# Both multi-head attentions of a four-layer gated network: head turns moved from TensorE to VectorE, the maxima's rows written by small DMAs

## The reference, cut to what matters

```
layer 0, feed-forward part: a mixture of M = 2 self-attentions (mha_wq/wk/wv/wo, biases bq, bk, bv, bo),
  for each m:  q = n1 @ wq + bq;  k = n1 @ wk + bk;  v = n1 @ wv + bv          (16 heads x 16)
               p = softmax(q k^T * scale);  o = (p v) @ wo + bo
  out = base + sum_m probs[m] * o_m        probs = softmax(mean over tokens of n1 @ rw + rb)
  then a router picks 2 of 8 experts for the batch
layer 2, cross attention: q from x, k and v from the context, keys masked (key_padding_mask),
  p = softmax(q k^T * scale + mask);  out = (p v) @ Wproj + bproj
```

## Time and profile before

| | |
|---|---|
| median of three executions | 3049.25 us |
| the profiled execution: span from first to last instruction | 3024.5 us |
| PE busy | 2799.0 us (93%) |
| DVE busy | 1718.6 us (57%) |
| ACT busy | 1210.0 us (40%) |
| POOL busy | 574.9 us (19%) |
| m0, first to last maximum | 190.8 to 962.4 us |
| a2, first to last maximum | 1745.4 to 2140.2 us |

### The profile page before, as it was taken

The page is one execution under the profiler, slowest core; times in us unless marked ns, Lnnn a source line. Parts: engine busy times, 40 slices in busy tenths (PEclk is TensorE's granted clock), DMA queues, the critical chain, the costliest instruction groups (busy, mean ns, idle before and its releaser), DMA issues. The chain is left out here.

```text
span 3024.5 us, 57684 instructions
## 1 busy us (share of the span) xinstructions
PE 2799.0 (93%) x20725; PEld 2241.0 (74%) x20726; DVE 1718.6 (57%) x4634; ACT 1210.0 (40%) x2332; POOL 574.9 (19%) x932
## 2 busy tenths in 40 slices
PE   7979999999999799899799689999799998978998
PEld 6856666666666688788688556666588887868998
DVE  5757777777775111588676477777322227861111
ACT  1225555555554111355335334445433224442221
POOL 1211111111110000011465411110011104561111
PEclk9989999999999899999799889999899999989999
DMA  3079800000000444100225400000211102025553
GB/s 124 0 263 393 316 0 0 0 0 0 0 0 1 145 152 147 42 22 15 88 80 158 132 29 22 21 21 0 65 56 56 56 0 77 15 95 192 175 186 117
DMA packets 126581, 246.66 MB, mean 82 GB/s; under 512 B 17132, under 2 KB 76780, under 8 KB 120048
## 3 DMA queue, kind: packets, MB, share of 16 engines
q1 hardware_dynamic: 116560, 219.59, 21.1%
q0 software_dynamic: 9888, 25.38, 2.4%
HBM read 149.01 MB, written 97.75 MB: 82 GB/s over the span
## 5 line engine op out<-in xcount | busy, mean ns | idle before, releaser
L537 DVE TENSOR_REDUCE m0hnm<-banks 128x4 f32<-128x1024 f32 x256 | 313.0, 1222 | 172.6 <-PE banks L465 172.5
L564 ACT ACTIVATE m0hpT<-banks 128x1024 f32<-128x1024 f32 x256 | 262.8, 1026 | 353.5 <-PE banks L478 353.5
L465 PE MATMUL banks<-m0hk,m0hq 32*128 32x256 f32 x2048 | 291.9, 403 | 12.2 <-DVE m0hnm L537 11.8
L478 PE MATMUL banks<-m0hq,m0hk 32*128 32x256 f32 x2048 | 289.9, 400 | 1.1 <-ACT m0hpT L564 1.1
L562 ACT ACTIVATE a2hpT<-banks,a2hlow 128x512 f32<-128x512 f32 x256 | 161.9, 684 | 194.3 <-PE banks L478 194.3
L465 PEld LDWEIGHTS banks<-m0hk,m0hq 32*128 32x128 f32 x2048 | 176.2, 185 | 63.9 <-DVE m0hnm L537 33.2
L537 DVE TENSOR_REDUCE a2hnm<-banks 128x4 f32<-128x1024 f32 x128 | 156.5, 1223 | 88.1 <-PE banks L465 88.1
L478 PEld LDWEIGHTS banks<-m0hq,m0hk 32*128 32x128 f32 x2048 | 177.3, 184 | 1.8 <-issue 1.4
L465 PE MATMUL banks<-a2hk,a2hq 32*128 32x256 f32 x1024 | 149.4, 410 | 21.7 <-DVE a2hnm L537 21.6
L3214 PEld LDWEIGHTS banks<-E3xT,E3w 128*128 128x128 f32 x1248 | 146.6, 194 | 2.4 <-DVE E3xT L3138 0.5
L478 PE MATMUL banks<-a2hq,a2hk 32*128 32x256 f32 x1024 | 146.5, 404 | 1.6 <-ACT a2hpT L562 1.5
(11 more groups left out here) (499 smaller groups left out, 6384.7 us busy)
## 6 DMA issues: line engine op xcount, KB each, us to landing
E3w<-in_L_ffn_W_dram SPq DMA_DIRECT2D x39, 1024.0 KB, 4.8
slots<-M0pad SPq DMA_DIRECT2D x8, 4290.0 KB, 33.8
slots_x<-M0pad SPq DMA_DIRECT2D x8, 4290.0 KB, 36.5
E0w<-in_L_ffn_fw_dram SPq DMA_DIRECT2D x64, 512.0 KB, 4.5
E2w<-in_L_ffn_w_dram SPq DMA_DIRECT2D x16, 1024.0 KB, 7.3
E1xin<-slots SPq DMA_DIRECT2D x71, 130.0 KB, 2.2
A2routed<-routed SPq DMA_DIRECT2D x16, 512.0 KB, 3.5
wide_all<-in_L_ffn_W_dram SPq DMA_DIRECT2D x8, 1024.0 KB, 8.7
```

The source lines that it names most:

```text
L465: ins = pe.matmul(self.scores[:, j, tc], self.q[strip(half, j), u, e, c, chunk(tc)], self.k[strip(half, j), u, e, c], start=True, stop=True)
L478: ins = pe.matmul(self.turned[:, j, kc], self.k[strip(half, j), u2, e2, c2, chunk(kc)], self.q[strip(half, j), u2, e2, c2], start=True, st ...
L537: v.tensor_reduce(self.nm[:, e, :, at:at + 33:32].rearrange("p c g -> p g c"), self.scores, AX.X, ALU.max, negate=True).then_inc(self.nm_r ...
L564: ins = a.activation(dst, self.turned, ACT.Exp)
```

## The change

- The maxima. `nm` shrinks to 32 columns for each chunk. After `highest(1)` DVE turns it in 32x32 blocks (`v.transpose`) to `nmT`, and SP issues four DMAs for each unit that write the four rows (two runs of 128 bytes each, four partitions a DMA) into q; in a2 a fifth DMA writes zeros into the mask's row of q. PE's `score_turned(1)` waits for the DMAs' semaphore. PE's turn (line 514) and DVE's addition (line 546) go.
- The pair's values. After the second weighted product DVE turns the bank `out` in 32x32 blocks straight to `raw` (128x512), takes the reciprocals of the sums from there, in m0 multiplies them by the attention's probability in an instruction of its own, multiplies 128x256 values, and a slot later turns the 128x256 result in 32x32 blocks to `onT`. PE's forward turns (line 524) and turn back (line 507), ACT's copies (lines 573 and 576) go. The order of the heads in the output weights is changed on the host to match.
- `take_v` moves from DVE to ACT. The value bias of m0 is no longer added there; four products at the start of m0 add `bv @ wo` to `bo` instead.
- The padding. `slots1` is written by SP during the first block (layer 0's cross attention), `slots_x` by ACT's queue in layer 1's cross attention, one DMA of 4290 KB in each of the first batches; m0's SP is free of them.
- Order on POOL: in m0 `norm2` comes before `make_base`; in a2 `copy_ctx` comes before `copy_low`.

```diff
+        self.nm, self.nmT = sb("hnm", [P, 2, C, 32]), sb("hnmT", [P, 2, C * 32])
+        self.raw, self.nrm, self.rec = sb("hraw", [P, 2, 8, 32]), sb("hnrm", [P, 8, 2, KD]), sb("hrec", [P, 2, 8])
+        self.qm_in = [sem_(tag + f"qm_in{i}") for i in range(4)]
+        self.put = 5 if masked else 4
...
             if half == 0:
                 pe.wait_ge(self.p_rdy, 2 * n2 + 1)
             else:
-                pe.wait_ge(self.qm_rdy, n2 + 1)
+                pe.wait_ge(self.qm_in[(i - 2) % 4], 16 * self.put * (job + (0 if i < 2 else 1)))
...
                 if not (first and i == 3):
-                    pe.wait_ge(self.nrm_rdy, 2 * job + (i - 3) // 2)
+                    pe.wait_ge(self.raw_rdy, 2 * job + (i - 3) // 2)
...
-        if i % 2 == 1 and (i >= 5 or not first):
-            pe.wait_ge(self.nrm_rdy, 2 * job + (i - 3) // 2)
-            for tc in range(C):
-                ins = pe.transpose(self.out[:, 1, chunk(tc)], self.nrm[:, tc], self.env.ident[:])
-            ins.then_inc(self.bk_mm, 1)
-        if old1:
...
-                ins = pe.transpose(self.top[:, chunk(tc)], self.nm[:, e1, tc], self.env.ident[:])
-            ins.then_inc(self.t_mm, 1)
...
-        if old3 and e3 == 1:
-            pe.wait_ge(self.raw_rdy, 2 * job + (i - 4) // 2 + 1)
...
-                    ins = pe.transpose(self.out[:, tc, chunk(h)], self.raw[:, h, chunk(tc)], self.env.ident[:])
-            ins.then_inc(self.fw_mm, 1)
...
-        if old1:
-            v.wait_ge(self.t_mm, n1 + 1)
-            v.tensor_tensor(self.q[:, u1, e1, c1], self.q[:, u1, e1, c1], self.top, ALU.add).then_inc(self.qm_rdy, 1)
         if new:
             highest(1)
+            v.wait_ge(self.nm_rdy, 2 * n + 2)
+            v.transpose(self.nmT[:, e], self.nm[:, e].rearrange("p c r -> p (c r)")).then_inc(self.nmT_rdy, 1)
...
-            a.activation(self.raw[:], self.out, ACT.Copy).then_inc(self.raw_rdy, 1)
...
-            a.activation(self.onT[:, (u if i >= 4 else 1 - u), (i - 5) % 4 // 2], self.out[:, 1], ACT.Copy).then_inc(self.on_rdy, 1)
...
+    def maxima(self, sp, job, u, i):
+
+        n, _, c, e = self.unit(job, u, i)
+        sp.wait_ge(self.nmT_rdy, n + 1)
+        row = 16 * (1 - e)
+        for j in range(4):
+            dst = self.q[row::32, u, e, c].rearrange("g (c x) -> g c x", c=C)[:, :, 32 * j:32 * j + 32]
+            sp.dma_start(dst, self.nmT[32 * j:32 * j + 32:8, e].rearrange("g (c x) -> g c x", c=C)).then_inc(self.qm_in[i], 16)
+        if self.masked:
+            sp.dma_start(self.q[row + 1::32, u, e, c], self.zero[:]).then_inc(self.qm_in[i], 16)
+
+    def sums(self, v, pair, weight=None):
+
+        v.wait_ge(self.av_mm, 2 * pair + 2)
+        v.transpose(self.raw[:].rearrange("p e s r -> p (e s r)"), self.out.rearrange("p e t -> p (e t)")).then_inc(self.raw_rdy, 1)
+        v.wait_ge(self.raw_rdy, pair + 1)
         if weight is None:
...
+            v.reciprocal(self.rec[:], self.raw[:, :, :, KD]).then_inc(self.inv_rdy, 1)
+            v.wait_ge(self.inv_rdy, pair + 1)
+            v.tensor_scalar(self.rec[:], self.rec[:], weight, None, ALU.mult).then_inc(self.rec_rdy, 1)
+
+    def normalise(self, eng, pair):
+
+        eng.wait_ge(self.rec_rdy, pair + 1)
+        eng.tensor_tensor(self.nrm[:].rearrange("p s e k -> p e s k"), self.raw[:, :, :, 0:KD],
+                          self.rec[:].unsqueeze(3).broadcast_to([P, 2, 8, KD]), ALU.mult).then_inc(self.nrm_rdy, 1)
+
+    def turn_back(self, v, pair, u, c):
+
+        v.wait_ge(self.nrm_rdy, pair + 1)
+        v.transpose(self.onT[:, u, c], self.nrm[:].rearrange("p s e k -> p (s e k)")).then_inc(self.on_rdy, 1)
+
+    def take_v(self, a, u, bank):
+
+        a.activation(self.v[:, u, :, :, 0:KD], bank.rearrange("p c (h k) -> p c h k", k=KD), ACT.Copy).then_inc(self.v_rdy, 1)
...
+            for job in range(2 * B):
+                for i in range(4):
+                    hd.maxima(sp, job, job % 2, i)
...
+            v.tensor_copy(bv_all[:], bv[:].unsqueeze(3).broadcast_to([P, 2, C, P])).then_inc(bv_rdy, 1)
+            v.wait_ge(bo_mm, 1)
+            v.tensor_tensor(bo[:], bo[:], env.bank(5), ALU.add).then_inc(bo_rdy, 1)
...
+                if b < 9:
+                    if b == 0:
+                        a.wait_ge(pad_rdy, 2)
+                    empty_region(a, w["slots_x"], b, pad, empty)
```

More of the change, by code:

```diff
@@ L266, in _ @@
             sp.dma_start(bv[:], rows(w["L0_xattn_bv"])).then_inc(w_in, 16)
+            sp.wait_ge(pad_rdy, 3)
+            for e in range(9):
+                empty_region(sp, w["slots1"], e, pad, empty)
+            sp.wait_ge(empty, 16 * 9)
         @block.gpsimd
@@ L448, in tensor @@
     def tensor(self, pe, job, u, i, first, fill=None):
-        new, old1, old2, old3 = self.parts(i, first)
+        new, _, old2, old3 = self.parts(i, first)
         n, _, c, e = self.unit(job, u, i)
-        n1, u1, c1, e1 = self.unit(job, u, i - 1)
         n2, u2, c2, e2 = self.unit(job, u, i - 2)
@@ L529, in vector @@
     def vector(self, v, job, u, i, first, mid=None, end=None):
-        new, old1, old2, old3 = self.parts(i, first)
+        new = self.parts(i, first)[0]
         n, _, c, e = self.unit(job, u, i)
-        n1, u1, c1, e1 = self.unit(job, u, i - 1)
         def highest(half):
             v.wait_ge(self.s_mm, 2 * n + half + 1)
-            at = 64 * half + 16 * (1 - e)
-            v.tensor_reduce(self.nm[:, e, :, at:at + 33:32].rearrange("p c g -> p g c"), self.scores, AX.X, ALU.max,
+            at = 16 * half
+            v.tensor_reduce(self.nm[:, e, :, at:at + 9:8].rearrange("p c g -> p g c"), self.scores, AX.X, ALU.max,
                             negate=True).then_inc(self.nm_rdy, 1)
@@ L552, in scalar @@
     def scalar(self, a, job, u, i, first, mid=None, end=None):
-        new, old1, old2, old3 = self.parts(i, first)
+        old2 = self.parts(i, first)[2]
         n2, u2, c2, e2 = self.unit(job, u, i - 2)
-        n3, u3, c3, e3 = self.unit(job, u, i - 3)
         def weights(half):
@@ L685, in _ @@
             weight(wv, "wv", 0, v_in)
-            for m in range(2):
-                sp.dma_start(bv[:, m], rows(w["L0_ffn_mha_bv"][m].rearrange("h k -> (h k)"))).then_inc(w_in, 16)
+            sp.dma_start(bv[:], w["L0_ffn_mha_bv"].rearrange("p (m c) -> p m c", m=2)).then_inc(w_in, 16)
             weight(wq, "wq", 1, w_in)
@@ L803, in take_q, with sums, turn_back @@
                 ins.then_inc(hd.q_rdy, 1)
-            def take_v(job, u):
-                v.wait_ge(v_mm, job + 1)
-                hd.take_v(v, u, G0, bv[:, u])
-            def normalise(pair, u):
-                hd.normalise(v, ch, pair, probs[:, u:u + 1])
+            def sums(pair, u):
+                hd.sums(v, pair, probs[:, u:u + 1])
+                hd.normalise(v, pair)
+            def turn_back(pair, u, c):
+                hd.turn_back(v, pair, u, c)
             def sum_up(b):
@@ L961, in take_k, with take_v @@
                 ins.then_inc(hd.k_rdy, 1)
+            def take_v(job, u):
+                a.wait_ge(v_mm, job + 1)
+                hd.take_v(a, u, G0)
             def rows1(b):
@@ L976, in at0 @@
                 def at0():
+                    take_v(2 * b, 0)
                     if not early:
@@ L1054, in _ @@
             pe.wait_ge(w_in, 16 * loads)
+            pe.wait_ge(bv_rdy, 1)
+            for m in range(2):
+                for k in range(C):
+                    ins = pe.matmul(env.bank(5)[:, m], bv_all[:, m, k], wo[:, m, k], start=(k == 0), stop=(k == C - 1))
+            ins.then_inc(bo_mm, 1)
             def body(b, first, early, last):
@@ L2119, in _ @@
             sp.dma_start(bp[:], rows(w["L2_xattn_bproj"])).then_inc(w_in, 16)
-            for b in range(1, B):
-                sp.wait_ge(high_in, 16 * b)
-                if b >= 2:
-                    sp.wait_ge(low_add, b - 1)
-                load_routed(b)
+            sp.wait_ge(high_in, 16)
+            load_routed(1)
+            for b in range(B):
+                if b + 2 < B:
+                    sp.wait_ge(high_in, 16 * (b + 2))
+                    sp.wait_ge(low_add, b + 1)
+                    load_routed(b + 2)
+                for i in range(4):
+                    hd.maxima(sp, b, b % 2, i)
         @block.gpsimd
@@ L2242, in job @@
                 start, more = first and u == 0, not (last and u == 1)
-                ch.start(2 if start else 3 * b - (1 if last and u == 1 else 0))
-                def mid0():
-                    take_v(b, u)
+                ch.start(b + 2)
                 def end0():
                     if not start:
-                        hd.normalise(v, ch, 2 * b - 2)
+                        hd.sums(v, 2 * b - 2)
+                        hd.normalise(v, 2 * b - 2)
                 def mid1():
+                    if not start:
+                        hd.turn_back(v, 2 * b - 2, 1 - u, 0)
                     if not first:
```

171 lines of the change are left out of this document (76 added, 95 removed).

## The result

The changed kernel takes 3078.51 us (median of four executions, 3073.86 to 3081.15), the kernel before, run beside it, 3050.29 us (3048.99 to 3052.04). The ratio is 1.0089, with a 95% interval of 1.0072 to 1.0107: the change makes the kernel 28 us slower. The forecast was 3036, faster; its range (3010 to 3092) holds the time, but its direction is wrong. That the range holds it is luck: its upper end came from slow turns, rival B, and the turns aren't slow.

The account below looks back on a forecast made before the run. PE's full share was taken to hide a loop through DVE, 2.46 us at least for half a slot. Terms: m0 +6, a2 -17, start +1.5, ends -4, together -13.5 us, giving 3036 us; range 3010 to 3092.

Parts of the forecast that it names:

- rival B: DVE's turns need two passes, 1.2 us for 512 columns: +40 in m0, +13 in a2 over the forecast, 3089; 15%.
- the model of the loop: Score product, DVE's reduction, next product into the same banks: at least 2.46 us a half, 4.92 a slot, whatever PE does.
- A: Full gain: PE is the bound throughout, so the turns taken off it save 143 us, time 2906; 3%.
- Rival C: The maxima's rows land late by DMA, 4.5 us each, so 192 slots wait 1 us on average: +190, 3226; 9%.
- step 1: On DVE after each second reduction, the turn of the maxima: 0.28 us more for each unit.
- m0's +0.42 a batch: Sum over m0's eight slots, slot 1's +1.15 the largest term; +6 us for 15 periods.
- `take_v` takes on ACT the place of the copy of `out`: 0: Slots 0 and 4: `take_v` leaves DVE, where DVE waited anyway, for ACT, at no cost.
- POOL's order: 0: The changed order of POOL's operations was given no cost.
- a2's -1.14 a job: Sum over a2's four slots, -0.49, -0.22, -0.21 and -0.22; -17 us for 15 periods.
- -4 us: At a stage's two ends a shorter chain replaces PE's turns and ACT's copies: -2 us each.
- the reason given: m0's start: a 512-wide copy (0.68) and four products with hand-overs come ahead of the first scores, +1.5 us.
- Rival D: DVE pays 0.1 more for each of five waits a pair, or ACT's issues aren't hidden: +10 to +20, 3050; 20%.

Follow-up runs that it names:

- ACT's order alone: The changed kernel with ACT's `rows1` put ahead of `take_v` in slot 4 of m0: 3087.78 us in one execution.
- POOL's order alone: The changed kernel with POOL's `make_base` and `keep` ahead of `norm2` in m0, as before the change: 3095.38 us in one execution.
- the pair alone: The changed kernel with the maxima's turn back on PE and their addition back on DVE: 3065.74 us, ratio 1.0052 to the kernel before.

## Why the prediction was wrong

**Right: the model of the loop.** A half can't be shorter than 2.46 us, and a slot's end on DVE lengthens the next half. Six of eight slots of m0 came within 0.1 us of it, slot 1 within 0.07 and its first half within 0.04. The prices of the turns were within 0.03. Rival B (slow turns) falls with them, though its time, 3089, is the nearest of all. A falls too: PE lost 69 us of busy time and nothing was gained. The Trainium skill, "VectorE: DVE Perf Modes", section "Rules for kernel authors", calls VectorE's turn the fastest for 32x32 blocks. The rows show it no faster by itself (0.67 us for 512 columns, against four turns of 128x128 in 0.66 on PE), only without the further pass over ACT. The kernel is slower all the same, since the time is counted on the engine that is late.

**Right: the rows' DMAs and the padding cost nothing.** No wait of PE for them, and even twice the DMAs cost nothing in the loop. Rival C falls. What the maxima's way does cost, 0.29 a job in a2, is of the size of step 1, DVE's turn.

**Wrong, and the largest part: m0's +0.42 a batch is +1.44.** Two terms failed, both put at nothing. They make 0.88 of the 1.02 that are missing, 13 of the 40 us between forecast and result.

1. "`take_v` takes on ACT the place of the copy of `out`: 0". In slot 4 ACT's `take_v` (0.59) is followed by what PE's fill waits for. I looked for who waits for `take_v` and not for who waits for what stands behind it. The term is +0.45, and ACT's order alone took it back (5.28 to 4.83).
2. "POOL's order: 0". The new order moves a copy of 0.60 us beside `apply2`, the last work of DVE ahead of a late reduction. The term is +0.43 in slot 7, where I had 0.65 for that step and it took 1.16; POOL's order alone took 0.42 of it back. Nothing in the prediction asks what DVE does while POOL works.

What remains, +0.20 over the other six slots, is small and partly of one kind. In slot 6 the eight products behind the forward turns took 1.89 (618.27 in the earlier trace rows) and take 2.00 without them; in slot 5 the score products, behind a wait of 0.30, take 1.24 where they took 1.16. A group of 0.49 that goes thus gives 0.39: some 0.1 of it had covered the start of the next.

**Mis-sized: a2's -1.14 a job is -0.77.** In the same way of reading, slot 0 gives 0.43 (0.49 forecast), slot 1 0.12 (0.22), slot 2 0.10 (0.21), slot 3 0.12 (0.22). The mechanism held; the terms lack 0.06 to 0.11 each, and over 15 jobs that is 6 of the 11 us by which the stage fell short.

**Not foreseen: the clock.** One batch in m0 and one or two jobs in a2 are 1.6 us longer, behind a fall of the granted clock. In the forecast nothing stood for it: +1.6 in m0 and +1.6 to +3.3 in a2. Why it falls there stays open. The rest of a2's difference is its first job, 27.1 to 30.9 us in three profiles of the kernel before and 29.7 and 30.9 in those of after.

**The ends.** -4 us were forecast at the two tails; +4 were measured (+0.5 and +3.8, means of two profiles that differ among themselves by up to 4 us, so that only the lack of a gain is sure). The chain there has less work in it, and why it isn't shorter is open. The granted clock in m0's tail is 0.62 and 0.63 in the two profiles after (990 to 1026, 991 to 1028 us) and 0.86, 0.68 and 0.79 in three before, so it may have a part.

**The start.** +1.6 was measured for +1.5, but not for the reason given. From SP's first issue in m0 to the first maximum it is 19.7 us in both later profiles before and 19.8 and 20.0 after: the chain of the bias is longer by about 1 us, and the padding's preparation, gone from there, gives about 0.7 back (19.0 with the padding alone moved). The rest lies in the block ahead of m0, and goes up and down by as much between two profiles of one kernel. That the sum is right is luck.

**The sum, in its own terms.** m0 +22 for +6, a2 -6 for -17, ends +4 for -4, start +1.6 for +1.5, layer 1's experts +3 and the rest +1 for 0: +26 for -13.5. Rival D (+10 to +20, 3050, 20%) is the nearest in kind, but its first half didn't happen: reciprocal and multiplication, which depend on each other, took 0.56 (635.10, 635.39, 635.66) where 0.49 was counted, not 0.1 more for each of five waits. Something on ACT wasn't hidden, as its second half says, but it was `take_v`, not the issues of the padding.

**The base was off too.** I took the first profile's 24.7 us "around the span" for the start and end of the program. In all later profiles it is 1.7. It did no harm to the difference, but a gap of that size was a sign that the profiled execution was not a usual one: its experts of layer 1 alone were 21 to 25 us shorter than in the next two profiles.

## What to carry to other kernels

Cost a move by what stands behind it on the engine that takes it, and who waits for that: 0.59 us in a place with "nothing to wait for" were half a microsecond of the critical path in each batch. When two engines form a loop, the change that pays is the one that takes work off the later of the two: moving the turns to DVE lost 0.9%; with 0.42 us of DVE's work for each pair on an idle POOL, the statistics and `finish` in free slots and two orders mended, the same design gained 0.6%, and 0.9% with the maxima left on PE. How much of that gain needs the turns on DVE at all isn't shown, since no run moves the statistics and `finish` in the kernel before. An estimate: before, slot 1's first half stands 0.33 above the floor (2.79), and moving `finish` gave 0.44 and 0.46 a job in the two kernels after (24.05 to 23.61, 23.76 to 23.30), so up to 5 and 7 of the 27 us (0.9%) could have been had without any turn moved. A line in the diff that only changes an order deserves the same look as one that adds an instruction.

## What the runs showed of the hardware

**TensorE's clock falls in some batches of the kernels in which PE waits more.** In the kernel before no batch in 600 to 950 us shows it. After, PE is busy for 310 of these 350 us instead of 348, and in the eleventh batch:

```profile
700.70 0.49 PE L488 MATMUL banks<-m0hk,m0hq 32*128 32x256 f32 x2 [1.72 <-DVE m0hnm L539]
701.87 3.68 PE L61 MATMUL banks<-M0n1T,M0wq 128*128 128x256 f32 x8
...
696.00:702.00 6.00, 3.99 (x53) 2.58 (x54) 5.15 (x16) 1.73 (x3) 0.91 (x2) 1.00 0.01 1
702.00:708.00 6.00, 5.70 (x44) 3.56 (x44) 4.30 (x11) 2.31 (x4) 0.89 (x2) 0.72 0.01 1
```

The last two rows are stretches: length, busy time of PE, its weight loads, DVE, ACT and POOL, then PE's granted clock. Behind a stretch in which PE was busy for 3.99 of 6 us the clock is 0.72 of its full 2.4 GHz on average, so that part of it ran at 1.2, and eight products take 3.68 us instead of 1.99. The batch is 1.6 longer, so a wait of PE may cost 1.6 more than its length. In the kernel with POOL's old order this befell eight batches of fifteen, in that with ACT's order six, in the one with the product on POOL none. The length of the waits alone doesn't decide it, since PE's waits for m0's maxima and for `n1T` come to 90 and 93 us in the first two, and to 93 in the kernel after with its one longer batch. A fall that comes elsewhere costs nothing. In four of the thirteen batches from 296 to 903 us it lies in slot 1, where DVE is later still; the sixteen products at 648.39 take 1.94 us, elsewhere 1.07, PE idles 0.36 behind them instead of 1.72, and the batches are equally long. Two of these places, the second with the fall:

```profile
596.00:601.00 5.00, 2.99 (x40) 1.91 (x44) 4.82 (x14) 1.70 (x2) 0.91 (x2) 1.00 0.01 1
646.00:651.00 5.00, 4.35 (x40) 2.27 (x44) 4.82 (x14) 1.70 (x2) 0.91 (x2) 0.66 0.01 1
```

What decides whether and where the clock falls isn't shown.

**Work on POOL slows DVE.** Two fp32 operations of 128x256 in SBUF take 0.73 us alone and 1.16 beside a 128x512 copy on POOL; the effect goes when the copy is moved. A product of two SBUF operands of 128x256 takes 0.42 alone and 0.85 beside that copy (the pair alone), and the two operations take 1.03 beside a product on POOL. On POOL that product takes 0.62, or 0.71 beside them, on DVE 0.42.

**One kernel's executions differ away from the edit.** Layer 1's experts took 268 us in one profile of the kernel before and 289 to 293 in two others of it.
